# Interleaving the first two hidden blocks by token halves, and splitting the first normalisation between VectorE and ScalarE

## The reference, cut to what matters

```python
xn = layernorm(x)                          # x: 2 x 4096 tokens of 256
x1 = ifft(fft(xn) * filt(D)).real          # D: a number from the first 1024 values of xn
lat = x1 @ W_el + b_el
bits = (lat > 0)
corrected = golay_correct(bits)            # per token, 24 bits
attn = x1 + corrected @ W_le + b_le
ffn = gelu(xn @ w1 + b1) @ w2 + b2         # 256 -> 1024 -> 256
return x + attn + ffn
```

## Time and profile before

| | us |
|---|---|
| median of 3 runs (lowest, highest) | 407.75 (407.51, 407.8) |
| the profiled execution | 407.3 |
| its span, first to last instruction | 405.5 |
| TensorE busy in it | 400.7 (99%) |
| VectorE / ScalarE / GpSimd busy | 298.7 / 223.3 / 87.2 |

### The profile page before, as it was taken

How to read it: one execution, slowest core, us unless ns; L and a number is a source line. 1 busy time by engine, 2 the same in 40 slices (tenths; PEclk the granted TensorE clock), 3 DMA queues, 4 the chain that set the end, 5 groups by cost and what they waited for, 6 DMA issues and landing times.

```text
span 405.5 us, 5548 instructions
## 1 busy us (share of the span) xinstructions
PE 400.7 (99%) x1774; PEld 329.1 (81%) x1774; DVE 298.7 (74%) x512; ACT 223.3 (55%) x333; POOL 87.2 (21%) x102
## 2 busy tenths in 40 slices
PE   8999999999999999999999999999999999999997
PEld 3888888888888888888888888888888888888886
DVE  5879985878658795677957788476974868757656
ACT  3967556557354664537545474554736556365561
POOL 3142421313003131121313013131121312113000
PEclk9999999999999999999999999999999999999999
DMA  6554333213333213333123332023333031111011
GB/s 187 218 158 156 104 103 106 63 42 104 103 104 98 44 65 103 104 103 97 46 64 104 103 104 90 26 91 103 104 103 78 40 89 53 54 52 52 2 52 52
DMA packets 15307, 35.75 MB, mean 88 GB/s; under 512 B 5440, under 2 KB 6592, under 8 KB 15296
## 3 DMA queue, kind: packets, MB, share of 16 engines
q1 hardware_dynamic: 15152, 35.49, 27.4%
q10 hardware_dynamic: 144, 0.13, 0.1%
HBM read 27.17 MB, written 8.45 MB: 88 GB/s over the span
## 4 chain that ended last, share of the span: by engine, by line
PE 97%; DMA 1%; DVE 1%; POOL 0%; SPq 0%; issue 0%
PE p_h L964 43%; PE p_f L982 28%; PE p_f L987 14%; PE p_s L1030 5%; PE p_l L1017 4%; PE p_s L1038 2%; DMA x_sb<-x 1%; PE p_f L997 0%; SPq L248 0%; DVE stats L830 0%; POOL row_nums L361 0%; DVE rows_sb L817 0%; PE p_g L1006 0%; PE p_l L1006 0%; PE p_s L1139 0%
## 5 line engine op out<-in xcount | busy, mean ns | idle before, releaser
L446 ACT ACTIVATE h<-p_h,small_sb 128x512 f32<-128x512 f32 x128 | 88.2, 689 | 139.4 <-PE p_h L964 138.9
L633 DVE TENSOR_TENSOR h_lo<-h,h_hi 128x512 fp32r<-128x512 f32 x128 | 102.9, 804 | 69.2 <-ACT h_hi L454 69.2
L982 PE MATMUL p_f<-h_hi,w_hi 128*128 128x512 f32 x252 | 98.3, 390 | 0.0
L982 PE MATMUL p_f<-h_hi,w_lo 128*128 128x512 f32 x252 | 98.1, 389 | 0.0
L369 POOL TENSOR_TENSOR uv<-xn 128x512 f32<-128x512 f32 x30 | 59.3, 1996 | 126.0 <-DVE xn L618 126.0
L454 ACT CAST h_hi<-h 128x512 fp32r<-128x512 f32 x128 | 79.5, 621 | 5.8
L964 PE MATMUL p_h<-xT_hi,w_hi 128*128 128x512 f32 (+1 forms) x258 | 79.4, 389 | 0.0
L964 PE MATMUL p_h<-xT_lo,w_hi 128*128 128x512 f32 (+1 forms) x258 | 79.2, 388 | 0.0
L964 PE MATMUL p_h<-xT_hi,w_lo 128*128 128x512 f32 (+1 forms) x258 | 79.0, 387 | 0.0
L987 PE MATMUL p_f<-h_lo,w_hi 128*128 128x512 f32 x252 | 77.6, 389 | 0.0
L964 PEld LDWEIGHTS p_h<-xT_lo,w_hi 128*128 128x128 f32 x258 | 48.3, 188 | 10.3 <-DVE xT_lo L839 0.2
(11 more groups left out here) (127 smaller groups left out, 325.2 us busy)
## 6 DMA issues: line engine op xcount, KB each, us to landing
xt_sb<-xt SPq DMA_DIRECT2D x16, 512.0 KB, 5.3
x_sb<-x SPq DMA_DIRECT2D x15, 512.0 KB, 4.6
rows_sb<-rows_dram SPq DMA_DIRECT2D x15, 512.0 KB, 4.4
out<-xt_sb SPq DMA_DIRECT2D x15, 512.0 KB, 2.8
xt_sb<-w SPq DMA_DIRECT2D x3, 512.0 KB, 7.5
xt_sb<-w SPq DMA_DIRECT2D x2, 256.0 KB, 4.5
x_sb<-x SPq DMA_DIRECT2D x2, 128.0 KB, 2.1
x_sb<-x SPq DMA_DIRECT2D x1, 256.0 KB, 3.2
```

The lines of the kernel that those rows point to most:

```text
L446: nc.scalar.activation(h[m % 2][:], p_h[:, m % 2, :], ACT.Gelu, bias=small_sb[:, S_B1 + m:S_B1 + m + 1]).then_inc(gelu_done, 1)
L633: nc.vector.tensor_tensor(h_lo[m % HR][:], h[m % 2][:], h_hi[m % HR][:].bitcast(F32), ALU.subtract).then_inc(h_lo_done, 1)
L982: mm(p_f[:, a, :], w[:, m, a * HF:(a + 1) * HF], h_hi[r][:], start=(m == 0 and w is w2_hi), stop=False, skip_group_check=True)
```

## The change: what it does, with the diff

- VectorE centres tiles 0 and 1 as soon as they are aggregated; ScalarE multiplies them by the reciprocal root, tile by tile. Tiles 2 and 3 are normalised on VectorE as before, behind w1's first low part.
- The identity is no longer loaded; GpSimd makes it from `ones` by a selection. Eleven idle products stand in front, one behind the first four transposes.
- Block 0 and block 1 are both made in token halves, with their products interleaved (`first_ups`); the transposes of a half go tile by tile.
- w1's first 256 KB are loaded and split in two pieces of one block each; ScalarE casts both before the hi part of the first tokens.
- On VectorE the statistics of chunk 1 go ahead of the low part of hidden block 1; on TensorE the product that sums the logarithms goes behind down block 2 instead of 1.

```diff
-W1_PARTS = ((0, 2), (2, 4), (4, 6), (6, MB))
-W1_LOADS = ((0, 2), (2, 4), (4, MB))
+W1_PARTS = ((0, 1), (1, 2), (2, 4), (4, 6), (6, MB))
+W1_LOADS = ((0, 1), (1, 2), (2, 4), (4, MB))
-IDLE = 12
+IDLE = 11
...
-            sp.dma_start(id_sb[:], ident).then_inc(id_in, 16)
+            sp.dma_start(small_sb[:], small).then_inc(small_in, 16)
             load_w1(0)
-            sp.dma_start(small_sb[:], small).then_inc(small_in, 16)
             load_w1(1)
+            load_w1(2)
             sp.dma_start(con[:], consts).then_inc(con_in, 16)
             load_w2(0)
             load_x(1)
-            load_w1(2)
+            load_w1(3)
...
+            pool.wait_ge(pool_set, 3)
+
+            nc.gpsimd.affine_select(out=id_sb[:], in_=ones[:], pattern=[[1, P]], base=0, channel_multiplier=-1,
+                                    compare_op=ALU.is_equal, fill=0.0).then_inc(id_made, 1)
             for q in range(2):
                 nc.gpsimd.memset(cw[q][:].bitcast(F32), 0.0).then_inc(cw_set, 1)
                 nc.gpsimd.memset(le2[q][:].bitcast(F32), 0.0).then_inc(le_set, 1)
-            pool.wait_ge(pool_set, 3)
...
+            act.wait_ge(rstd_done, 1)
+            for j in range(HALF):
+                act.wait_ge(centred0, j + 1)
+                nc.scalar.mul(xn0[:, j, :], xn0[:, j, :], row_nums[0][:, 1, j:j + 1]).then_inc(scaled0, 1)
             w1_part_hi(0)
+            w1_part_hi(1)
             for g in range(2):
                 act.wait_ge(t0_done, g + 1)
                 nc.scalar.copy(half_tokens(xT_hi[0], g), half_bank(g)).then_inc(t0_hi, 1)
-            w1_part_hi(1)
+            w1_part_hi(2)
...
             aggregate(0, range(HALF))
+
+            dve.wait_ge(stat_done, 1)
+            for j in range(HALF):
+                nc.vector.tensor_scalar(xn0[:, j, :], x_sb[0][:, j, :], mv[0][:, j, 0:1], None,
+                                        ALU.subtract).then_inc(centred0, 1)
             dve.wait_ge(x_in[0], 16)
...
-            for g in range(2):
-                normalise(g)
             w1_part_lo(0)
+            dve.wait_ge(rstd_done, 2)
+            for j in range(HALF, CT):
+                nc.vector.tensor_scalar(xn0[:, j, :], x_sb[0][:, j, :], mv[0][:, j, 0:1], row_nums[0][:, 1, j:j + 1],
+                                        ALU.subtract, ALU.mult).then_inc(xn0_done, 1)
             for g in range(2):
                 dve.wait_ge(t0_hi, g + 1)
                 nc.vector.tensor_tensor(half_tokens(xT_lo[0], g), half_bank(g), half_tokens(xT_hi[0], g).bitcast(F32),
                                         ALU.subtract).then_inc(t0_lo, 1)
+                if g == 0:
+                    w1_part_lo(1)
...
-            w1_part_lo(1)
+            w1_part_lo(2)
...
-            w1_part_lo(2)
-            hidden_lo(0, 1)
+            w1_part_lo(3)
             statistics(1, 1)
             dve.wait_ge(stats_made, 3)
             aggregate(1)
+            hidden_lo(0, 1)
             hidden_lo(0, 2)
...
+            def turn_rows(g, ready):
+
+                for j in range(HALF):
+                    pe.wait_ge(ready, j + 1)
+                    for k in range(KB):
+                        last = nc.tensor.transpose(half_bank(g)[:, k, j * P:(j + 1) * P],
+                                                   xn0[:, g * HALF + j, k * P:(k + 1) * P], id_sb[:])
+                last.then_inc(t0_done, 1)
+
+            def half_up(m, g, terms, last_term=2):
+
+                tok = slice(g * GTOK, (g + 1) * GTOK)
+                for n in terms:
+                    w, xp = ((w1_hi, xT_hi), (w1_lo, xT_hi), (w1_hi, xT_lo))[n]
+                    for k in range(KB):
+                        last = mm(p_h[:, m, tok], w[:, k, m * P:(m + 1) * P], xp[0][:, k, tok],
+                                  start=(n == 0 and k == 0), stop=(n == last_term and k == KB - 1), skip_group_check=True)
+                return last
+
+            def first_ups():
+
+                turn_rows(0, scaled0)
+                mm(p_f[:, 0, :], idle[:, 0:P], idle[:], start=True, stop=True)
+                pe.wait_ge(t0_hi, 1)
+                for m in range(2):
+                    pe.wait_ge(w1_hi_ready, m + 1)
+                    half_up(m, 0, (0,))
+                turn_rows(1, xn0_done)
+                pe.wait_ge(w1_ready, 1)
+                half_up(0, 0, (1,))
+                pe.wait_ge(t0_lo, 1)
+                half_up(0, 0, (2,))
+                half_up(1, 0, (2,), last_term=1)
+                pe.wait_ge(w1_ready, 2)
+                half_up(1, 0, (1,), last_term=1)
+                pe.wait_ge(t0_hi, 2)
+                half_up(0, 1, (0, 1))
+                half_up(1, 1, (0, 1))
+                pe.wait_ge(t0_lo, 2)
+                half_up(0, 1, (2,)).then_inc(up_done, 1)
+                half_up(1, 1, (2,)).then_inc(up_done, 1)
...
-            pe.wait_ge(id_in, 16)
-            for g in range(2):
...
-                pe.wait_ge(xn0_done, g + 1)
...
+            pe.wait_ge(id_made, 1)
             pe.wait_ge(pool_set, 3)
-            for m in range(LOOK):
+            first_ups()
+            for m in range(2, LOOK):
                 up(0, 0, m, first=True)
...
-                if m == 1:
+                if m == 2:
                     summed_over(16, 1, fr_d[:, 0:1], logged, dim_made)
```

More of the change, by code:

```diff
@@ L62, with build @@
 S_END = S_WEL + KB * LAT
-def build(nc, x, xt, small, latent, w1, w2, ident, consts, basis, out):
+def build(nc, x, xt, small, latent, w1, w2, consts, basis, out):
     ctx = ExitStack()
@@ L176, in build @@
         w2_in = [sem(f"w2_in{i}") for i in range(len(W2_LOADS))]
-        id_in, con_in, basis_in, small_in = sem("id_in"), sem("con_in"), sem("basis_in"), sem("small_in")
+        id_made, con_in, basis_in, small_in = sem("id_made"), sem("con_in"), sem("basis_in"), sem("small_in")
         latent_in, stored = sem("latent_in"), sem("stored")
@@ L190, in build @@
         veps_done, rstd_done, mean_done = sem("veps_done"), sem("rstd_done"), sem("mean_done")
-        xn0_done, t0_done, t0_hi, t0_lo = sem("xn0_done"), sem("t0_done"), sem("t0_hi"), sem("t0_lo")
+        centred0, scaled0, xn0_done, t0_done, t0_hi, t0_lo = sem("centred0"), sem("scaled0"), sem("xn0_done"), sem("t0_done"), sem("t0_hi"), sem("t0_lo")
         fr_taken, xc0_made = sem("fr_taken"), sem("xc0_made")
@@ L525, in _ @@
             hidden_hi(0, 1, first=True)
-            w1_part_hi(2)
+            w1_part_hi(3)
             gelu(0, 2, first=True)
@@ L529, in _ @@
             w2_part_hi(1)
-            w1_part_hi(3)
+            w1_part_hi(4)
             gelu(0, 3, first=True)
@@ L811, in w2_part_lo @@
                                         ALU.subtract).then_inc(w2_ready, 1)
[L813 to L819, removed]
             for j in range(HALF):
@@ L874, in _ @@
                                     ALU.add).then_inc(logged, 1)
-            w1_part_lo(3)
+            w1_part_lo(4)
             w2_part_lo(1)
@@ L945, in up @@
                     if first and m == m0:
[L947 to L966, removed]
@@ L967, in up @@
-                last.then_inc(up_done, 1)
+                        pe.wait_ge(w1_ready, n + 1)
+                pe.wait_ge(gelu_done, MB * c + m - 1)
+                n = 0
+                for w, xp in ((w1_hi, xT_hi), (w1_lo, xT_hi), (w1_hi, xT_lo)):
+                    for k in range(KB):
+                        last = mm(p_h[:, m % 2, :], w[:, k, m * P:(m + 1) * P], xp[par][:, k, :],
+                                  start=(n == 0), stop=(n == 3 * KB - 1))
+                        n += 1
@@ new lines, in up @@
+                last.then_inc(up_done, 1)
+            def turn_rows(g, ready):
[9 more added lines that the diff above has]
+                    w, xp = ((w1_hi, xT_hi), (w1_lo, xT_hi), (w1_hi, xT_lo))[n]
+                    for k in range(KB):
+                        last = mm(p_h[:, m, tok], w[:, k, m * P:(m + 1) * P], xp[0][:, k, tok],
+                                  start=(n == 0 and k == 0), stop=(n == last_term and k == KB - 1), skip_group_check=True)
+                return last
@@ L1219, in constants @@
     assert a.sum(axis=1).min() >= 4
-    return np.eye(P, dtype=f4), con, basis
+    return con, basis
 def layouts(inputs):
@@ L1255 @@
     arrays = {name: np.ascontiguousarray(a) for name, a in layouts(inputs).items()}
-    for name, a in zip(("ident", "consts", "basis"), constants()):
+    for name, a in zip(("consts", "basis"), constants()):
         arrays[name] = a
```

## The result

The changed kernel takes 409.44 us (median of 6, 409.33 to 410.13) against 407.59 (median of 6 of the kernel before on the same chip): ratio 1.0049, 95% interval 1.0036 to 1.0062, or 1.85 us slower. The forecast was 408.45 with a range of 407.4 to 409.4. The profiled execution took 409.47, its span is 407.7, 2.2 us over the one before.

A forecast was written before the change was run, and what follows sets the result against it. Bound: the start of TensorE's unbroken products at up block 3, held by products and ScalarE's gelu chain. Terms -0.23, +1.07, -0.08 give +0.76, said +0.7 on 407.75: 408.45 us, range 407.4 to 409.4.

The forecast's parts named there:

- the start: Up to up block 3 of chunk 0: first product 0.23 us earlier, but block 3 at 13.95 instead of 13.19, +0.76 us.
- Behind that point: After up block 3: later statistics and the moved product cost 0; filter weights at 28.1, cover before the circulant 0.1 us.
- 0.3 longer: Before the circulant: if POOL's or VectorE's part is 0.3 us longer, the thin cover becomes a stall, kept for the range.
- The w1 load: Landing kept at 7.05, bounds 5.2 and 7.56; token cast waits for both w1 casts; first product at 8.11, 0.23 us earlier.
- rival (a): w1 load lands early, at 6.5: first product 7.5, block 3 at 13.4, +0.2, 407.95 us; chance 0.12.
- The up blocks: Interleaved blocks 0 and 1: block 0 complete at 11.3, gelu 0 0.84 us later, TensorE idle 0.8, block 3 at 13.95.
- The second wait: TensorE before up block 3: idle 0.2 us or more, ended by ScalarE's gelu 1.
- Centring and scaling: First two tiles: centring 4.05 to 4.79 moves nothing behind it on VectorE; ScalarE scales from 5.16, tiles at 5.66 and 6.06.
- The selection on GpSimd: Making the identity on GpSimd: 0.5 us taken, bounds 0.16 and 2.0, over by 4.0; cost 0.
- rival (c): TensorE's clock rises later, products of 256 columns at 0.22 us: up to +3.2, 410.9 us, or +1.7, 409.4; chance 0.08.
- Rival (b): The start alone counts: gelus are not the bound, the stream begins 0.2 to 0.5 us earlier, 407.4 us; chance 0.1.
- The statistics' order: VectorE takes chunk 1's statistics before hidden block 1's low part; covered with a microsecond of slack, cost 0.

The follow-up runs named there:

- Run 3: Changed kernel, with VectorE waiting for the filter weights before it centres and scales chunk 1; 409.05 us, ratio 1.0041 to the kernel before.
- run 1: Changed kernel, with the product that sums the logarithms back behind down block 1; 407.99 us, ratio 1.0011 to the kernel before.
- run 2: Kernel before, with only the product that sums the logarithms moved behind down block 2; 408.94 us, ratio 1.0039 to the kernel before.
- run 7: Run 4's kernel, with ScalarE's second w1 cast behind the first token cast; 407.38 us, ratio 0.9998 to the kernel before.
- run 4: Run 1's kernel, with block 0's products before block 1's wherever their operands are there; 407.59 us, ratio 1.0002 to the kernel before.
- run 8: Run 1's kernel, without the idle product behind the first transposes; 407.87 us, ratio 1.0024 to the kernel before.
- run 5: Run 1's kernel, with chunk 1's statistics back behind the low part of hidden block 1; 408.0 us, ratio 1.0021 to the kernel before.

## Why the prediction was wrong

**The bound and the sign were right, the sum too small**: +0.7 was forecast, +1.85 measured. Two terms missed in opposite directions, the start by 0.4 too much and the circulant by 1.7 too little, so that the total missed by less than the circulant did is luck.

**The step that failed** is in "Behind that point", which was put at "Cost 0, by this cover": "Filter weights: 26.20 + 1.9 = 28.1 ... So the cover is down to 0.1". The delay was right (the chain starts 2.18 later, of which 0.4 is the start's own). The chain's length was carried over as 5.2 us, and it measured 7.22, because the delay moved its second half from a stretch in which VectorE waited for the rows of chunk 1 into one in which it centres and scales 1024 columns. Run 3 shows it: same lateness, 5.05 us, no wait. In the place of 0 the circulant's wait measured 1.59 us. Runs 1 and 2 show that the product makes the difference in both kernels. The sentence on a part "0.3 longer" saw the thin cover but bounded it far too tightly: four operations can each be held by a VectorE operation of up to 1.2 us.

**The w1 load.** Taken at 7.05; ScalarE found both pieces there and cast them without a pause from 6.35. With that the sentence that the token cast waits for ScalarE's w1 casts and not for the transposes fell too: both end together (run 7). The start came out as rival (a), which had the chance 0.12: it said a landing at 6.5, the first product at 7.5, block 3 at 13.4 and +0.2; measured are 7.62, 13.54 and +0.35, of which 0.12 is the later first product. From the first product to block 3 the forecast itself had 13.95 - 8.11 = 5.84, and 5.92 was measured: products of 256 columns stand 0.12 apart here (half of 9.58 - 9.34), where 0.11 was taken, over 24 of them 0.24, and the rest of the sum had about that much too much.

**The up blocks.** The wait for gelu 0 was forecast at 0.8 and measured 0.69; from gelu 0 to up block 3 it is 13.54 - 11.04 = 2.50, where the sum has 2.55. The mechanism stands, and run 4 prices it at 0.4 to 0.5. The second wait, "0.2 or more before block 3", is not in the list, but block 3 does follow gelu 1, by 0.05 (12.81 + 0.68 = 13.49), in run 4 as well (12.77 + 0.68 = 13.45, and 13.50). It starts 0.21 after the small product in front of it (13.33), where before it started 0.14 after it (13.05), so the wait is about 0.07. In the kernel before, gelu 1 ended 0.18 ahead of block 3, and products set its start; that block 3 waited for it there was not so.

**Centring and scaling.** The scaling of two tiles took 0.91 (5.54 to 6.45), 0.39 later than forecast; two tiles at 0.5 with 0.4 between starts were right. The root was later: the second tile of x landed later and the aggregation ended 0.26 later (4.26, not 4.00), and the addition of eps on GpSimd behind it took 0.35 instead of 0.20, ending 0.05 after the first centring of VectorE (4.29, 0.35), under which it began (0.35 in runs 1 and 7, too).

```profile
4.34 0.35 POOL L359 TENSOR_TENSOR var_eps<-mv,eps 128x2 f32<-128x2 f32 x1 [1.90 <-DVE mv L604]
```

So "nothing behind them on VectorE moves" was right of the centrings and not enough: they also stood in GpSimd's way. The selection on GpSimd took 0.29 (0.5 taken, bounds 0.16 and 2.0), at no cost.

**The clock, rival (c)**: no. In the changed kernel the idle product behind the transposes already takes 0.38 instead of the 0.44 spacing and 0.63 length of a cold one. In run 8's profile it wasn't needed, with the reserve told there. The Trainium skill, page TensorE: Matmul & The Clock Gate, section Part 4: PE-mode transpose, says that transposes don't count in the same way. No run here tests it: the eleven products ahead of them may have earned the rise. **Rival (b)** was right only in that the start is 0.7 earlier; none of it reached block 3. **The statistics' order**: cost 0, as forecast (run 5).

What remains over the kernel before without the moved product is 0.4 to 1.0 us by the ratios of runs 1, 5 and 8 (1.0011 to 1.0024). Block 3's 0.35 lies just under its lower end; the rest isn't resolved by these intervals.

## What to carry to other kernels

An engine's operations keep their length only as long as they have the same company. When a step is moved, lay the whole chain that hangs on it over the other engine's timeline at its new time; a cover worked out from old durations is worth little once GpSimd's small operations come to lie under VectorE's long ones with two SBUF inputs. And work that is pulled forward on the busiest engine gains nothing if it stands in front of what another engine's serial chain waits for: here block 1's products delayed block 0, and with it two gelus, by some 0.5 us (run 4).

## What was not expected of the hardware

Beside the GpSimd operations held by VectorE, once even under a centring, which has a single input tensor in SBUF (L359 above), one more. In the profiled execution of run 2, behind the wait of 1.79 us, TensorE's clock fell to its lower level. The windows view (us, busy PE, PEld, DVE, ACT, POOL, granted clock, DMA share, GB/s):

```profile
31.00:32.00 1.00, 1.00 (x6) 0.82 (x6) 0.33 (x1) 1.00 (x3) 0.00 (x0) 0.77 0.72 250
32.00:33.00 1.00, 1.00 (x4) 0.81 (x3) 1.00 (x2) 0.49 (x2) 0.00 (x0) 0.50 1.03 410
...
35.00:36.00 1.00, 1.00 (x6) 0.82 (x5) 0.52 (x1) 0.97 (x3) 0.00 (x0) 1.00 0.77 311
```

The granted clock was 0.50, 1.2 GHz, for about 3.5 us, after the products had resumed at 30.46; products of 512 columns then stand 0.42 apart (31.55 to 31.97) instead of 0.23. The span is 408.8, 3.3 over the kernel before, where the median is only 1.7 over. The changed kernel's profiled execution, with a wait of 1.59, kept 1.00 throughout. The execution took 410.6, 1.7 over the median of its run, and is the only one of twelve with a lower mean clock (0.996). That the wait brought the fall about is not shown: one execution of the kernel before had a mean clock of 0.996 and 409.27 us, and two of run 8 were like it, and the profiles of these kernels show no such wait. What is shown is the price: some 3.5 us at the lower level go with about 1.7 us more.
